# Scores by row quarters and a late division in a chain's cross attention (one NeuronCore)

## The chip, the cores and the metric

One core of a Trainium2 chip runs the whole program in one launch. The metric is device time in microseconds (us), from the first to the last instruction on that core with what lies around them; lower is better. The kernel before takes 2385.2 us in the median of three runs.

## The reference, cut to what matters

Four layers work on `x` of 2 x 1024 tokens and 256 channels, with a context of 2 x 64 tokens and 192 channels. The change lies in layer 0, in its cross attention with 16 heads of 16 channels:

```python
h = _layernorm(x, ln2_w, ln2_b)
q = (h @ q_w + q_b).reshape(B, T, H, HD).transpose(0, 2, 1, 3)
k = (enc @ k_w + k_b).reshape(B, S, H, HD).transpose(0, 2, 1, 3)
v = (enc @ v_w + v_b).reshape(B, S, H, HD).transpose(0, 2, 1, 3)
attn = jnp.einsum('bhtd,bhsd->bhts', q, k) * scale
attn = jnp.where(enc_mask[:, None, None, :], neg, attn)
attn = jax.nn.softmax(attn, axis=-1)
ca = jnp.einsum('bhts,bhsd->bhtd', attn, v).transpose(0, 2, 1, 3).reshape(B, T, C)
x = x + ca @ out_w + out_b
h = _layernorm(x, ln3_w, ln3_b)
h = jax.nn.gelu(h @ mlp1_w + mlp1_b, approximate=False)
x = x + h @ mlp2_w + mlp2_b
```

Here B is 2, T 1024, S 64, C 256, H 16, HD 16. Everything is float32.

## The kernel before

The program runs in parts, one behind another. `part_chain0` (L1065) computes everything between the first self attention and the second one: cross attention, MLP, a routing attention over the 64 context tokens, gates and norms. It works in four blocks; a block is 256 tokens (two tiles `t` of 128 tokens) of each of the two batch rows, which are two streams `s`. `chain_blocks` writes the first and last block out and loops over the middle two. Each stream has its own PSUM tile `ch.ps[s]` of 128 x 2048 floats, which is four banks of 512, so that PSUM is full. Each engine runs its instructions in the order written (`emit` in each engine's block) and waits on semaphores for named steps of other engines (`after`, L784). So the order of the work is the order of the code, on each engine for itself.

One block's cross attention, step by step:

- `head` (L1100, TensorE): turns the norm's output, multiplies by `q_w` (L1109); ScalarE adds the bias and keeps `qT` (L1332). Then the scores (L1117): for each tile `t` and channel half `g` one product of 128 rows with `e.kbd`, 512 columns wide. `kbd` holds the keys of 8 heads side by side, block by block on the diagonal: head `h` of the half uses the rows 16h to 16h+15 and the columns 64h to 64h+63, and everything else is zero. Behind each product a one-instruction product adds the mask's rows (`add_bias`, L876). The steps are `ca.scores0` and `ca.scores1`, one for each tile.
- `cross_vector` (L968, VectorE): for each stream and tile, the maximum over 64 keys per head (L987, "top") and the subtraction (L989, "less"), and one tile later the sums of the exponentials (L976, "total") and their reciprocal, 128 x 16 (L979, "inverse"). Last it copies the turned probabilities of stream 1 out of PSUM (L996, `turned_kept`).
- `cross_scalar` (L1004, ScalarE): the four exponentials (L1009), then the copy of stream 0's turned probabilities (L1012).
- `cross_gpsimd` (L1017, GpSimd): multiplies each tile's exponentials by the reciprocals (L1023, "probs").
- `cross` (L1131, TensorE): in this order `turn(0)`, `values(0)`, `turn(1)`, `projected(0)`, `values(1)`, `projected(1)`. `turn` is 16 transposes into all four banks (L1136). `values` is eight products (L1143), each on 32 columns of the array, four of which run side by side. ScalarE copies the result to `caT` (L1342), and `projected` multiplies it by `o_w` (L1152) and adds a bias row.
- VectorE then runs `finish_block(i - 1)` (the last norm of the block before, L806 to L846; not in block 0), and only then adds the projection to `x` (`ca.x`, L1031) and makes the norm `n3`, with two small steps on GpSimd; TensorE turns it (L883) and starts the MLP (L1217, L1224).

A float32 product shows as two MATMUL records, so the eight products of `values` are 16 records. Of scores and transposes the counts are to be read the same way (a transpose is one record).

## Time and profile before

| | us |
|---|---|
| median of three runs | 2385.2 (2384.72 to 2385.51) |
| the profiled execution, device time | 2383.92 |
| its span, first to last instruction | 2382.2 |
| first chain (blocks 0 to 3), about | 449 to 875 |
| one middle block | 105 |
| mean granted TensorE clock | 0.943 |

PE is TensorE's products, PEld its weight loads, DVE VectorE, ACT ScalarE, POOL GpSimd. Times in the trace are from the start of the span. In a row of the timeline the first number is the start, the second the time that the instructions of the row cover together, then engine, line, operation, output<-input, shapes, count, and in brackets how long the engine had been idle before it and who ended that. The granted clock is given as a share of TensorE's full 2.4 GHz; 0.50 is 1.2 GHz.

### The profile page before, as it was taken

Reading aid. Unit: us, or ns where it says so; the run is one execution under the profiler, and the core shown is the slowest. Engines: PE = TensorE matmul, PEld = TensorE weight load, DVE = VectorE, ACT = ScalarE, POOL = GpSimd, SP = SyncE. Lnnn points to the kernel's source line nnn. Section 1 sums busy time; section 2 is a strip of 40 time slices with the busy share of each in tenths; the row PEclk is TensorE's granted clock in tenths of the full one; section 3 lists DMA queues with packets and bytes.
Section 4 is the critical chain, followed back from the end, with each engine's and each line's share of the span. In section 5 each row is a group of like instructions: output and inputs, shape, how many; then the busy total and the mean of one; then the engine's idle time right before and its main releaser. Section 6 shows DMA issues by size and latency. Waiting matters only on the chain. (4 is left out here: it accounts for less than half of the span.)

```text
span 2382.2 us, 27289 instructions
## 1 busy us (share of the span) xinstructions
PE 2086.4 (88%) x10510; PEld 1203.7 (51%) x10550; DVE 1130.7 (47%) x2031; ACT 933.0 (39%) x1435; POOL 777.5 (33%) x508
## 2 busy tenths in 40 slices
PE   2789998487979767999999999999998979898987
PEld 1444444275757554433343335334433857576766
DVE  5476672435252435455535554555450152525343
ACT  2256665133333322555545553554454422121211
POOL 3211100013032121566646664666466010202011
PEclk8899999699989887999999999999999989899989
DMA  5723320400000004000000000000000500000000
GB/s 121 130 37 44 42 29 2 113 1 0 1 0 0 1 1 122 1 1 1 1 1 1 1 1 1 1 2 1 1 2 1 161 27 1 9 1 9 0 9 9
DMA packets 48266, 52.77 MB, mean 22 GB/s; under 512 B 14730, under 2 KB 39052, under 8 KB 47732
## 3 DMA queue, kind: packets, MB, share of 16 engines
q1 hardware_dynamic: 48148, 51.17, 10.3%
q8 instruction: 77, 1.26, 0.2%
q14 instruction: 41, 0.34, 0.1%
HBM read 41.31 MB, written 8.80 MB: 21 GB/s over the span
## 5 line engine op out<-in xcount | busy, mean ns | idle before, releaser
L1731 POOL TENSOR_TENSOR total<-total,pr 128x1024 f32<-128x1024 f32 x192 | 465.1, 2423 | 241.9 <-ACT pr L1872 229.0
L1872 ACT ACTIVATE pr<-sc 128x1024 f32<-128x1024 f32 x256 | 260.0, 1022 | 355.3 <-PE sc L1651 355.3
L1752 DVE TENSOR_REDUCE pmax<-ring 128x1 f32<-128x512 f32 x512 | 325.9, 685 | 133.9 <-PE ring L1618 125.8
L1669 PE MATMUL o<-pr,v_pair 128*64 128x512 f32 x1024 | 275.7, 617 | 1.2
L1651 PE MATMUL sc<-q_full,k_full 64*128 64x512 f32 x1024 | 267.2, 591 | 0.0
L522 ACT ACTIVATE probs<-s 128x512 f32<-128x512 f32 (+1 forms) x304 | 163.2, 575 | 101.5 <-PE s L309 55.0
L1618 PE MATMUL ring<-k_round,q_round 64*128 64x512 f32 x512 | 185.0, 598 | 5.3 <-DVE pmax L1752 4.3
L1023 POOL TENSOR_TENSOR c_scores<-c_scores,c_total 128x1024 f32<-128x1024 f32 (+1 forms) x48 | 77.0, 1616 | 344.5 <-DVE c_total L979 344.5
L1618 PEld LDWEIGHTS ring<-k_round,q_round 64*128 64x128 f32 x512 | 74.4, 188 | 155.1 <-DVE pmax L1752 97.2
L394 DVE TENSOR_REDUCE row_max<-s 128x1 f32<-128x640 f32 (+3 forms) x128 | 127.3, 1020 | 47.3 <-PE s L291 47.1
L1669 PEld LDWEIGHTS o<-pr,v_pair 128*64 128x64 f32 x1024 | 51.2, 134 | 144.4 <-issue 142.6
L1731 POOL TENSOR_TENSOR total<-pr 128x1024 f32<-128x1024 f32 x32 | 75.3, 2353 | 141.8 <-ACT pr L1872 141.8
L2166 PE MATMUL c_ps<-c_hT,hT 128*128 128x256 f32 x512 | 117.3, 392 | 4.4 <-ACT c_hT L898 4.4
L288 PE MATMUL s<-k_stack,q_stack 128*128 128x512 bf16 (+3 forms) x367 | 92.9, 328 | 30.3 <-DMA k_stack<-mask_dram 16.7
L898 ACT ACTIVATE c_hT<-c_ps,c_ln_b,c_ln_g 128x256 f32<-128x256 f32 x64 | 32.4, 561 | 213.2 <-PE c_ps L883 213.2
L948 PE MATMUL c_ps<-vw,c_pT 128*128 128x256 f32 x384 | 100.0, 421 | 13.3 <-ACT c_pT L1012 13.3
L2166 PEld LDWEIGHTS c_ps<-c_hT,hT 128*128 128x128 f32 x512 | 100.2, 197 | 19.7 <-ACT c_hT L898 5.4
L1648 PE MATMUL sc<-shift,picks 64*128 64x512 bf16 x512 | 104.8, 387 | 4.8 <-DMA shift<-top_dram 4.8
L827 POOL TENSOR_TENSOR c_rstd<-c_moments,eps 128x2 f32<-128x2 f32 x48 | 9.4, 196 | 304.2 <-DVE c_moments L811 304.2
L1651 PEld LDWEIGHTS sc<-q_full,k_full 64*128 64x128 f32 x1024 | 104.6, 192 | 6.9
L306 PE MATMUL s<-q_stack,k_stack 128*128 128x512 bf16 (+3 forms) x361 | 99.3, 325 | 1.2 <-ACT probs L522 0.9
L948 PEld LDWEIGHTS c_ps<-vw,c_pT 128*128 128x128 f32 x384 | 79.8, 213 | 28.4 <-ACT c_pT L1012 15.3
(285 smaller groups left out, 3430.1 us busy)
## 6 DMA issues: line engine op xcount, KB each, us to landing
qk_dram<-qk_parts SPq DMA_DIRECT2D x32, 192.0 KB, 3.1
q_stack<-qk_dram SPq DMA_DIRECT2D x48, 128.0 KB
k_stack<-qk_dram SPq DMA_DIRECT2D x48, 128.0 KB
x<-in_x SPq DMA_DIRECT2D x4, 512.0 KB, 7.3
mlp_w<-in_L_xattn_mlp_w SPq DMA_DIRECT2D x2, 1024.0 KB, 8.1
wq<-in_L_xattn_Wq SPq DMA_DIRECT2D x2, 1024.0 KB, 6.6
wo<-in_L_xattn_Wo SPq DMA_DIRECT2D x2, 1024.0 KB, 14.9
hT<-in_L_xattn_ff_w SPq DMA_DIRECT2D x1, 2048.0 KB, 19.0
```

The lines of the kernel that those rows point to most:

```text
L306: ins = te.matmul(dst[:, x * width:(x + 1) * width], k[:, j, kt * P:(kt + 1) * P], q[:, j, c0:c0 + width], start=True, stop=not diagonal)
L394: dve.tensor_reduce(row_max[:, heads[0], t:t + 1], src[:, 0:(t + 1) * P], AX.X, ALU.max).then_inc(s1_free, 1)
L522: act.activation(probs[at % KEPT][:, heads[0]:heads[-1] + 1, 0:width], s2[u % RING][:, 0:len(heads) * width].rearrange("p (j q) -> p j q", ...
L948: ins = te.matmul(dst, ch.pT[s][:, c, t * P:(t + 1) * P], vw[:, s, c, :], start=c == 0, stop=c == cols // P - 1 and out_bias is None)
L1618: te.matmul(ring[i % RING][:], qr[head[j], t * P:(t + 1) * P], kr[head[j], halves[half]], start=True, stop=True).then_inc(s1_made, 1)
L1648: te.matmul(s2[at % 2][:, j], picks[head[j]], shift[n % 2][head[j], halves[half]], start=True, stop=False)
L1651: ins = te.matmul(s2[at % 2][:, j], kf[n % 2][head[j], keys], qf[n % 2][head[j], halves[half]], start=False, stop=True)
L1669: ins = te.matmul(o[64 * j:64 * j + 64], v[n % 2][:, kt, 64 * j:64 * j + 64], probs[(U * n + u) % KEPT][:, j], start=kt == 0, stop=kt == T ...
L1731: pool.tensor_tensor(out=total[half][:], in0=other[:], in1=probs[at % KEPT][:], op=ALU.add).then_inc(sums, 1)
L1752: dve.tensor_reduce(part_max[:, j, t, half:half + 1], ring[i % RING][:], AX.X, ALU.max).then_inc(s1_free, 1)
L1872: act.activation(probs[here % KEPT][:], s2[at % 2][:], ACT.Exp).then_inc(s2_free, 1)
L2166: ins = te.matmul(ch.ps[s][:, 1024 * part + 256 * f:1024 * part + 256 * (f + 1)], w.f1[:, k, chunk * P:(chunk + 1) * P], ch.hT[s][:, k, :] ...
```

## The change

The scores are computed by row quarters. The 32 rows of quarter `r` hold two heads, whose keys fill 128 columns of `kbd`; the rest of the columns is zero for these rows. Each product of 128 rows and 512 columns becomes four products of 32 rows and 128 columns, one for each quarter `r`, and each quarter writes into its own bank `r` of the stream. The mask's rows are added behind all of them, once for each bank. There is one step `ca.scores` for the four banks in place of two; VectorE reads a tile's 16 heads across all four banks.

The division moves behind the values. VectorE makes no sums over the exponentials and GpSimd multiplies nothing. TensorE turns the bare exponentials, and `values` issues, beside the eight products with the values, eight more with a constant `sums_of`, which put each head's sum on that head's 16 rows, in the third bank. VectorE, behind its copy of stream 1, takes the reciprocal of these 128 x 512 sums and multiplies the 128 x 512 values by it; that is the new `caT`, and ScalarE's copy (L1342) goes. `turn(s)` now waits for "less" of both tiles and the exponential in place of "probs". All of this stands ahead of `finish_block(i - 1)` on VectorE.

```diff
--- before.py
+++ after.py
@@ -651,6 +651,10 @@
         @block.vector
         def _(dve):
             dve.memset(e.vcol[:], 0.0).then_inc(zeroed, 1)
+            dve.memset(e.sums_of[:], 0.0).then_inc(zeroed, 1)
+            dve.wait_ge(zeroed, 2)
+            for x in range(2):
+                dve.memset(e.sums_of[S2 * x:S2 * x + S2, 16 * x:16 * x + 16], 1.0)
...
-            dve.wait_ge(zeroed, 1)
             dve.wait_ge(pe.sem, pe.value("v"))
...
@@ -960,12 +963,15 @@
     return ch.scores[s][:].rearrange("p t n -> p (t n)")[:, 0:2 * cols].rearrange("p (t n) -> p t n", t=2)
 
 
-def cross_vector_steps(name):
+def cross_vector_steps(name, sums=True):
+    if not sums:
+        return [f"{name}.{x}" for x in ("top0", "less0", "top1", "less1", "turned_kept")]
     return [f"{name}.{x}" for x in ("top0", "less0", "top1", "less1", "total0", "inverse0", "total1", "inverse1",
                                     "turned_kept")]
 
 
-def cross_vector(dve, ch, name, i, cols):
+def cross_vector(dve, ch, name, i, cols, quarters=False, sums_made=True):
+
 
     heads = cols // S2
     by_head = lambda ap: ap.rearrange("p (h k) -> p h k", k=S2)
@@ -982,16 +988,23 @@
     last = None
     for s in range(B):
         for t in range(2):
-            src, top = by_head(ch.ps[s][:, t * cols:(t + 1) * cols]), ch.top[s][:, t, 0:heads]
-            after(dve, ch.te[s], f"{name}.scores{t}", i)
+            if quarters:
+                src = ch.ps[s][:].rearrange("p (r t h k) -> p r t h k", r=4, t=2, k=S2)[:, :, t]
+                top = ch.top[s][:, t, 0:heads].rearrange("p (r h) -> p r h", r=4)
+                less, tops = sc(s, t).rearrange("p (r h) k -> p r h k", r=4), top.unsqueeze(3).to_broadcast([P, 4, 4, S2])
+            else:
+                src, top = by_head(ch.ps[s][:, t * cols:(t + 1) * cols]), ch.top[s][:, t, 0:heads]
+                less, tops = sc(s, t), top.unsqueeze(2).to_broadcast([P, heads, S2])
+            after(dve, ch.te[s], f"{name}.scores" + ("" if quarters else str(t)), i)
             dve.tensor_reduce(top, src, AX.X, ALU.max).then_inc(ch.dve[s].sem, ch.dve[s].one(f"{name}.top{t}"))
             after(dve, ch.dve[s], f"{name}.top{t}", i)
-            dve.tensor_tensor(out=sc(s, t), in0=src, in1=top.unsqueeze(2).to_broadcast([P, heads, S2]),
-                              op=ALU.subtract).then_inc(ch.dve[s].sem, ch.dve[s].one(f"{name}.less{t}"))
-            if last:
+            dve.tensor_tensor(out=less, in0=src, in1=tops, op=ALU.subtract).then_inc(
+                ch.dve[s].sem, ch.dve[s].one(f"{name}.less{t}"))
+            if last and sums_made:
                 sums(*last)
             last = (s, t)
-    sums(*last)
+    if sums_made:
+        sums(*last)
     after(dve, ch.te[1], f"{name}.turned", i)
     dve.tensor_copy(ch.pT[1][:, 0:cols // P, :].rearrange("p c n -> p (c n)"), ch.ps[1][:, 0:2 * cols]).then_inc(
         ch.dve[1].sem, ch.dve[1].one(f"{name}.turned_kept"))
@@ -1065,16 +1078,16 @@
 def part_chain0(nc, e, A):
     with ExitStack() as ctx:
         w = e.w0
-        te_steps = ["n2.T", "ca.q", "ca.scores0", "ca.scores1", "ca.turned", "ca.v", "ca.out", "n3.T", "mlp.up", "mlp.down", "n4.T", "rt.scores",
+        te_steps = ["n2.T", "ca.q", "ca.scores", "ca.turned", "ca.v", "ca.out", "n3.T", "mlp.up", "mlp.down", "n4.T", "rt.scores",
                     "rt.turned", "rt.routed", "n5.T", "gates", "cand"]
-        dve_steps = (norm_steps("n2") + cross_vector_steps("ca") + ["ca.x"] + norm_steps("n3")
+        dve_steps = (norm_steps("n2") + cross_vector_steps("ca", False) + ["ca.inverse", "ca.vT", "ca.x"] + norm_steps("n3")
 ...
-        act_steps = ["n2.hT", "ca.qT", *cross_scalar_steps("ca"), "ca.vT", "n3.hT", "mlp.gelu",
+        act_steps = ["n2.hT", "ca.qT", *cross_scalar_steps("ca"), "n3.hT", "mlp.gelu",
                      "x.T", "n4.hT", "rt.exp", "rt.kept", "n5.hT",
                      "r", "u", "tanh"]
         ch = Chain(nc, ctx, "c0", te_steps, dve_steps, act_steps,
-                   ["n2.shifted", "n2.rstd", "ca.probs0", "ca.probs1", "n3.shifted", "n3.rstd", "n4.shifted",
+                   ["n2.shifted", "n2.rstd", "n3.shifted", "n3.rstd", "n4.shifted",
                     "n4.rstd", "n5.shifted", "n5.rstd"], e.biases0.shape[1])
...
+        inverse = ch.sb("inverse", [P, 512])
@@ -1098,8 +1112,8 @@
         @block.tensor
         def _(te):
             def head(i, rows_later=None):
-                scores = lambda s, t, g: ch.ps[s][:, 1024 * t + 512 * g:1024 * t + 512 * (g + 1)]
-                masked = lambda s, t, g: add_bias(te, ch, scores(s, t, g), 4 * C + 512 * s)
+                bank = lambda s, r: ch.ps[s][:, 512 * r:512 * (r + 1)]
+                masked = lambda s, r: add_bias(te, ch, bank(s, r), 4 * C + 512 * s)
                 for s in range(B):
                     turn_step(te, ch, e, i, "n2", s)
                 for s in range(B):
@@ -1112,26 +1126,31 @@
                     ins.then_inc(ch.te[s].sem, ch.te[s].one("ca.q"))
                 for s in range(B):
                     after(te, ch.act[s], "ca.qT", i)
+
                     for t in range(2):
                         for g in range(KC):
-                            te.matmul(scores(s, t, g), qT[s][:, g, t * P:(t + 1) * P], e.kbd[:, s, g, :],
-                                      start=True, stop=False)
-                            if rows_later is None:
-                                ins = masked(s, t, g)
-                        if rows_later is None:
-                            ins.then_inc(ch.te[s].sem, ch.te[s].one(f"ca.scores{t}"))
+                            for r in range(4):
+                                rows = slice(32 * r, 32 * r + 32)
+                                te.matmul(bank(s, r)[:, (2 * t + g) * P:(2 * t + g + 1) * P],
+                                          qT[s][rows, g, t * P:(t + 1) * P],
+                                          e.kbd[rows, s, g, P * r:P * r + P], start=t + g == 0, stop=False)
+                    if rows_later is None:
+                        for r in range(4):
+                            ins = masked(s, r)
+                        ins.then_inc(ch.te[s].sem, ch.te[s].one("ca.scores"))
                 if rows_later is not None:
                     te.wait_ge(ch.rows_made, rows_later)
                     for s in range(B):
-                        for t in range(2):
-                            for g in range(KC):
-                                ins = masked(s, t, g)
-                            ins.then_inc(ch.te[s].sem, ch.te[s].one(f"ca.scores{t}"))
+                        for r in range(4):
+                            ins = masked(s, r)
+                        ins.then_inc(ch.te[s].sem, ch.te[s].one("ca.scores"))
 
             def cross(i):
                 def turn(s):
                     for t in range(2):
-                        after(te, ch.pool[s], f"ca.probs{t}", i)
+
+                        after(te, ch.dve[s], "ca.less1", i)
+                        after(te, ch.act[s], f"ca.exp{t}", i)
                         for c in range(8):
                             ins = te.transpose(ch.ps[s][:, c * 256 + t * P:c * 256 + (t + 1) * P],
                                                ch.scores[s][:, t, c * P:(c + 1) * P], e.ident[:])
@@ -1139,13 +1158,19 @@
 
                 def values(s):
                     after(te, (ch.act, ch.dve)[s][s], "ca.turned_kept", i)
+                    for g in range(KC):
+                        for r in range(4):
+                            ins = te.matmul(ch.ps[s][32 * r:32 * r + 32, 256 * g:256 * (g + 1)],
+                                            e.vcol[:, s, 4 * g + r, :], ch.pT[s][:, 2 * r + g, :],
+                                            start=True, stop=True)
+
                     for c in range(8):
-                        ins = te.matmul(ch.ps[s][32 * (c % 4):32 * (c % 4) + 32, 256 * (c // 4):256 * (c // 4 + 1)],
-                                        e.vcol[:, s, c, :], ch.pT[s][:, c, :], start=True, stop=True)
+                        ins = te.matmul(ch.ps[s][32 * (c % 4):32 * (c % 4) + 32, 1024 + 256 * (c // 4):1280 + 256 * (c // 4)],
+                                        e.sums_of[:], ch.pT[s][:, 2 * (c % 4) + c // 4, :], start=True, stop=True)
                     ins.then_inc(ch.te[s].sem, ch.te[s].one("ca.v"))
 
                 def projected(s):
-                    after(te, ch.act[s], "ca.vT", i)
+                    after(te, ch.dve[s], "ca.vT", i)
                     for t in range(2):
                         dst = ch.ps[s][:, 512 + t * C:512 + (t + 1) * C]
                         for g in range(KC):
@@ -1281,7 +1306,13 @@
                 if first:
                     head(0)
                     assert bias_rows(dve, ch, e.biases0, PIECE) == ROWS_MADE
-                cross_vector(dve, ch, "ca", i, 1024)
+                cross_vector(dve, ch, "ca", i, 1024, quarters=True, sums_made=False)
+                for s in range(B):
+                    after(dve, ch.te[s], "ca.v", i)
+                    dve.reciprocal(inverse[s][:], ch.ps[s][:, 1024:1536]).then_inc(*one(s, "ca.inverse"))
+                    after(dve, ch.dve[s], "ca.inverse", i)
+                    dve.tensor_tensor(out=caT[s][:].rearrange("p g t -> p (g t)"), in0=ch.ps[s][:, 0:512],
+                                      in1=inverse[s][:], op=ALU.mult).then_inc(*one(s, "ca.vT"))
                 if not first:
                     finish_block(i - 1)
                 for s in range(B):
@@ -1338,10 +1369,6 @@
                     head(0)
                 cross_scalar(act, ch, "ca", i, 1024)
                 for s in range(B):
-                    after(act, ch.te[s], "ca.v", i)
-                    act.activation(caT[s][:].rearrange("p g t -> p (g t)"), ch.ps[s][:, 0:512],
-                                   ACT.Identity).then_inc(*one(s, "ca.vT"))
-                for s in range(B):
                     after(act, ch.te[s], "n3.T", i)
                     turned_scalar(act, ch, s, 0, ch.hT[s], w.vec["ln3_g"], w.vec["ln3_b"]).then_inc(*one(s, "n3.hT"))
                 for s in range(B):
@@ -1401,7 +1428,6 @@
             def emit(i, first, last):
                 if first:
                     norm_gpsimd(pool, ch, e, "n2", 0)
-                cross_gpsimd(pool, ch, "ca", i, 1024)
                 if not first:
                     norm_gpsimd(pool, tail, e, "n6", i - 1)
                 for name in ("n3", "n4", "n5"):
@@ -2324,6 +2350,7 @@
         front = ctx.enter_context(ExitStack())
         fb = lambda n, s, d=F32: front.enter_context(nc.sbuf_tensor(n, s, d))
         e.kbd, e.vcol = fb("kbd", [P, B, KC, 512]), fb("vcol", [P, B, 8, 32])
+        e.sums_of = fb("sums_of", [P, 32])
         e.q_w, e.q_bs, e.o_w = fb("q_w", [P, KC, C]), fb("q_bs", [P, KC]), fb("o_w", [P, KC, C])
 
         e.biases0 = fb("biases0", [P, 4 * C + B * 512])
```

## Rows read from the trace of the kernel before

**Rows 1.** The page's busy time of TensorE and its share of the span
```profile
PE 2086.4 (88%) x10510; PEld 1203.7 (51%) x10550; DVE 1130.7 (47%) x2031; ACT 933.0 (39%) x1435; POOL 777.5 (33%) x508
```
**Rows 2.** Windows (length; busy PE, PEld, DVE, ACT, POOL; clock; DMA), blocks 0 and 1
```profile
488.30:573.50 85.20, 78.95 (x389) 61.56 (x388) 31.64 (x82) 30.54 (x65) 16.46 (x23) 1.00 0.00 1
...
573.50:583.80 10.30, 6.16 (x37) 4.08 (x35) 6.38 (x8) 4.65 (x5) 5.66 (x3) 0.50 0.00 0
...
594.00:604.20 10.20, 5.82 (x15) 4.52 (x16) 4.37 (x18) 1.02 (x2) 1.79 (x4) 0.50 0.01 2
```
**Rows 3.** Timeline of PE, block 1, from the first score to the MLP
```profile
562.50 1.02 PE L1117 MATMUL c_ps<-kbd,c_qT 128*128 128x512 f32 x2
563.36 0.38 PE L876 MATMUL c_ps<-c_rows,c_ones 96*128 96x512 bf16 x1
...
573.18 1.64 PE L1136 MATMUL c_ps<-ident,c_scores 128*128 128x128 f32 x8 [1.89 <-POOL c_scores L1023]
...
580.93 1.93 PE L1143 MATMUL c_ps<-c_pT,vcol 128*32 128x256 f32 x16 [2.03 <-ACT c_pT L1012]
582.80 2.44 PE L1136 MATMUL c_ps<-ident,c_scores 128*128 128x128 f32 x16
585.07 1.03 PE L1152 MATMUL c_ps<-o_w,c_caT 128*128 128x256 f32 x4
...
587.62 1.07 PE L1143 MATMUL c_ps<-c_pT,vcol 128*32 128x256 f32 x16 [0.43 <-DVE c_pT L996]
...
597.27 1.11 PE L883 MATMUL c_ps<-ident,c_h 128*128 128x128 f32 x4 [5.65 <-DVE c_h L818]
```
**Rows 4.** Timeline of DVE, block 1: two maxima, copy, start of finish_block, ca.x
```profile
564.86 1.23 DVE L987 TENSOR_REDUCE c_top<-c_ps 128x16 f32<-128x1024 f32 x1 [6.79 <-PE c_ps L876]
...
567.26 1.22 DVE L987 TENSOR_REDUCE c_top<-c_ps 128x16 f32<-128x1024 f32 x1
...
585.27 2.29 DVE L996 COPY c_pT<-c_ps 128x2048 f32<-128x2048 f32 x1 [5.25 <-PE c_ps L1136]
587.49 0.42 DVE L806 BATCH_NORM_STATS2 c_t_stats<-c_xc 128x6 f32<-128x256 f32 x1
...
593.63 0.69 DVE L1031 TENSOR_TENSOR x<-c_ps,x 128x512 f32 x1
```
**Rows 5.** Timeline of ACT, block 1: the last exponential, the copy of stream 0
```profile
577.27 1.06 ACT L1009 ACTIVATE c_scores<-c_scores 128x1024 f32<-128x1024 f32 x1 [2.69 <-DVE c_scores L989]
578.94 1.94 ACT L1012 ACTIVATE c_pT<-c_ps 128x1024 f32<-128x1024 f32 x2 [0.61 <-PE c_ps L1136]
```
**Rows 6.** Groups by form, whole span: VectorE's reciprocals
```profile
L979 DVE RECIPROCAL c_total<-c_total 128x16 f32<-128x16 f32 x32 | 8.1, 253 | 1.1
...
L979 DVE RECIPROCAL c_total<-c_total 128x8 f32<-128x8 f32 x16 | 3.3, 203 | 0.6
L1302 DVE RECIPROCAL c_rtotal<-c_rtotal 128x2 f32<-128x2 f32 x8 | 1.3, 166 | 6.1 <-ACT c_rp L1363 6.1
```
**Rows 7.** Groups by form, first chain alone: what the change removes
```profile
L1023 POOL TENSOR_TENSOR c_scores<-c_scores,c_total 128x1024 f32<-128x1024 f32 x16 | 30.3, 1902 | 56.8 <-DVE c_total L979 56.8
```
**Rows 8.** Timeline of PE: short products, each with its own weight load
```profile
631.68 1.00 PE L1173 MATMUL c_ps<-tokT,c_xT 128*128 128x64 f32 x8
```
**Rows 9.** Weight loads in narrow windows: four column tiles; two row halves (L1651)
```profile
484.27 0.19 PEld L1143 LDWEIGHTS c_ps<-c_pT,vcol 128*32 128x32 f32 x4 [0.23 <-issue]
...
1303.33:1303.53 0.20, 0.20 (x2) 1.00 0.00 0
```
**Rows 10.** Timeline of block 0: the mask's rows, copies of both streams, ca.x
```profile
467.13 1.90 PE L876 MATMUL c_ps<-c_rows,c_ones 96*128 96x512 bf16 x8 [0.45 <-DVE c_rows L862]
...
481.85 1.94 ACT L1012 ACTIVATE c_pT<-c_ps 128x1024 f32<-128x1024 f32 x2 [0.61 <-PE c_ps L1136]
...
488.92 2.29 DVE L996 COPY c_pT<-c_ps 128x2048 f32<-128x2048 f32 x1 [5.99 <-PE c_ps L1136]
...
491.13 0.68 DVE L1031 TENSOR_TENSOR x<-c_ps,x 128x512 f32<-128x512 f32 x1
```

## The prediction

> **What bounds the kernel now.** I read the page first: TensorE is busy 88% of the span [rows 1], so time is mostly won by taking work from it or by closing its gaps. Then the windows of the first chain, where the change lies: its granted clock is full over 85 us of block 0, but in each middle block two stretches of 10 us stand at half, the 1.2 GHz level [rows 2]. The timeline shows what lies ahead of them. TensorE is idle for 1.89 us on GpSimd's multiplication, then 2.03 us on ScalarE's copy; and 5.65 us before the MLP on the norm `n3` [rows 3]. So in the cross attention TensorE is not the bound. The bound is a chain across the engines: scores, softmax on VectorE, exponential, division, turn, copy, values, projection, `ca.x`, norm. Its end is the turn of `n3` at 597.27. VectorE sets that end, because it runs in the order of the code: the copy of stream 1 at 585.27, then `finish_block` from 587.49, then `ca.x` at 593.63 [rows 4]. What I ask of every part of the change is where it puts `ca.x`. Behind it the block goes on as before.
>
> **The change part by part, in a middle block** (times of block 1, 558.95 to 664).
>
> *Scores.* Before, a pair of records takes 0.86 us from its start to the mask product behind it and each mask product 0.22 us more (562.50, 563.36, the next pair at 563.58) [rows 3]. After, a stream has 16 products, 32 records, four of them on different rows of the array. If four run side by side it is eight waves. A wave has 128 columns and a load of its own; the nearest row is eight short products with loads, 1.00 us, so 0.125 us each [rows 8]: 1.0 us in place of 3.44. With four mask products stream 0 is readable at 562.50 + 1.00 + 3 x 0.22 + 0.42 = 564.6, where VectorE began at 564.86 [rows 4]. That is a gain of 0.3 us and no more, because before VectorE needed only the first tile's half. The 4.9 us saved on the two streams turn into idle time. Bounds for the 32 records: 1.0 us (side by side) to 4.0 us (32 x 0.125, one behind another); I take 1.0, since two loads on different row halves fit into 0.20 us together and four on different columns into 0.19 us [rows 9].
>
> *Softmax.* A maximum and a subtraction take 2.40 us (564.86 to 567.26) [rows 4]. Four pairs, with no sums between them, end at 564.6 + 9.6 = 574.2. The last exponential, 1.06 us [rows 5], ends at 575.4. GpSimd's 16 multiplications of 1.90 us [rows 7] go, four of them from each block, and half of those from the path. ScalarE's copy for stream 0 stands behind all four exponentials in its queue, so it ends at 575.4 + 1.94 = 577.4, against 580.9 [rows 5]. This is what the change gains: 3.5 us.
>
> *Values and sums.* At half clock eight products take 1.87 us from the start to the turn behind them (580.93 to 582.80), at full clock 1.07 [rows 3]. The sums are eight more of the same shape. TensorE now idles from about 566 to 569.5 and from 572 to 577.4, longer than the gaps that led to the half clock before, so I take 2 x 1.87 = 3.7: 581.1. The turn of stream 1 takes 2.3 (582.80 to 585.07) [rows 3]: 583.4 against 585.1. The copy on VectorE takes 2.29 [rows 4]: 585.7.
>
> *Reciprocal.* It now works on 512 elements per partition. The rows show 2 elements in 166 ns, 8 in 203, 16 in 253 [rows 6]: 6.2 ns for each further element, over both steps. 253 + 496 x 6.2 ns = 3.33 us. Bounds: 0.69 us, what a plain operation on 128x512 out of PSUM takes (593.63) [rows 4], if the cost did not grow; and 4.0, one such pass on top. I take 3.33, since three sizes lie on one line. With the multiplication, 0.69, it is 4.0 us for a stream: stream 0 has its `caT` at 589.7. On VectorE this replaces nothing; what it replaces is ScalarE's copy. The Trainium skill, VectorE: DVE Perf Modes ("First, the fixed hardware budget"), says that the reciprocal is an iterative divide with a repeat count of 8. Taken as eight cycles of the page's 0.96 GHz for each element, my estimate by that page is 4.27 us and the sum below would be 7.5 us larger; the rows here show 6.2 ns, not 8.3.
>
> *What is queued behind the new waits.* TensorE's order is `turn(1)`, `projected(0)`, `values(1)`, `projected(1)`. Before, ScalarE made `caT(0)` at once and `projected(0)` ran under VectorE's copy. Now VectorE makes it behind that copy, so TensorE waits from 583.4 to 589.7, and `values(1)` waits behind `projected(0)`. Two times 1.03 us [rows 3] is 2.1; a gap of 6.3 us is longer than the one before the MLP, so I take half clock, 4.1: 593.8. Values and sums of stream 1 at full clock again, 1.9: 595.7. Reciprocal and multiplication, 4.0: 599.7. VectorE is in order, so `finish_block` starts only here, in place of 587.49. It takes 6.14 us (587.49 to 593.63) [rows 4]: `ca.x` at 605.9, 12.3 us later than before. `projected(1)` is hidden under it.
>
> *Behind `ca.x`.* Before, the half-clock stretch ended at 604.2 [rows 2], 10.6 us behind `ca.x`. After, TensorE has worked until shortly before (`projected(1)` at 600 to 604), so that stretch should sit a little earlier; I give back 1.1 us. GpSimd's queue has only the norms' small steps left and delays nothing. A middle block costs +11.2 us, and the last one, which has `finish_block(2)` ahead of `ca.x` too, the same: 3 x 11.2 = 33.6.
>
> *Block 0.* It has no `finish_block` at this place. VectorE can begin when four mask products, not two, are through: 467.13 + 0.42 + 3 x 0.22 = 468.2 [rows 10]; +9.6 + 0.1 + 1.06 + 1.94 = 480.9, against 483.8. Values and sums 3.7, turn 2.7 (between the clocks), copy 2.3: 489.6. Then 4.0, projection 3.1, values and sums 2.8, 4.0: 503.5. `ca.x` was at 491.13 [rows 10]: +12.4. Its MLP ran at full clock from the start [rows 2]; after a gap of 4 us under the second reciprocal part of it will not: +1.5. Block 0: +13.9.
>
> *The rest.* The three memsets of `sums_of` lie under loads of weights (price if not: below 0.3 us). The parts behind the chain shift as a whole.
>
> The sum: 33.6 + 13.9 = +47.5 us against the profiled execution's 2383.9, whose span is 2382.2: 2431.4. The median of the runs is 1.3 above that execution, and I forecast **2432 us**.
>
> **The rivals.**
>
> *The row quarters do not run side by side.* Then the stream's scores take 4.0 us in place of 1.0, VectorE begins 3.0 us later in blocks 1 to 3 (block 0's scores are hidden behind the bias rows): +9, 2441 us. For it: the pair of rows with two loads shows that they were in flight together, not that 128 columns of four were. Against it: [rows 9]. The Trainium skill, TensorE: Matmul & The Clock Gate ("LDWEIGHTS (loading the stationary operand)"), says that a load's time goes by its columns, so that 32 rows take as long as 128; that alone would be this rival, but its section on packing small matmuls lets loads on different rows overlap.
>
> *The reciprocal is dearer,* 4.0 us, since it reads PSUM, which no reciprocal of this length here does: eight times 0.67, 2437 us.
>
> *The reciprocal is cheap.* At 0.69 us, eight times 2.64 us fall away from the sum: 21.1 less, 2411 us. For it: no row has a long reciprocal. Against it: three sizes on a line. Even then the order on VectorE keeps it slower.
>
> *The clock stays full: the other side.* The place is TensorE's wait before `values(0)`. If the clock did not fall there or at `projected(0)`, my sum's own half-clock terms go, 1.9 + 2.0 us a block, some 15 in all, and the two old stretches with 6.16 and 5.82 us of busy time at half [rows 2] give up to 6.0 us back in three blocks, 18. With the cheap reciprocal that is 2432 - 21 - 15 - 18 = 2378 us, faster than before; with the reciprocal at 3.33 it would still be about 2399. It decides only if idle gaps of 5 us leave the clock alone and the reciprocal is below about 1.5 us. Against it: gaps of 2 us led to half clock [rows 2, 3].
>
> **How the numbers follow.** A measurement of this kernel can tell about 0.2%, 4.8 us, from no change. Chances: my forecast 0.76, quarters one behind another 0.10, dearer reciprocal 0.06, cheap reciprocal 0.06, full clock with cheap reciprocal 0.02. The forecast's own range is 2422 to 2441: each block has some 2 us of half clock that may fall otherwise. The range takes in the dearer cases and leaves out the last two: 2419 to 2444. Only the last is not slower, and between it and 2390 lies little: faster 0.02, same 0.01, slower 0.97.
>
> **What the changed profile would show.** A RECIPROCAL on 128x512, eight times, near 3.3 us; under 1 us would make me wrong by 20 us. Score records of 32 rows starting in fours, and the two streams through in under 4 us. The first value product about 3.5 us earlier behind the last score than before. TensorE's gap before `projected(0)` near 6 us, released by the multiplication on VectorE. `ca.x` some 12 us later in the block, block length about 116 us. If `ca.x` is not later, the forecast fails; if it is later by 5 us only, the reciprocal was mis-sized.

## The result and the profile after

The changed kernel takes 2434.55 us in the median of four runs (2432.26 to 2436.1), against 2385.11 for the kernel before: ratio 1.0206, 95% interval 1.0194 to 1.0218. It is slower by 49 us. The profiled execution took 2432.26 us, with a span of 2430.4 and a mean granted clock of 0.935 (0.943 before).

The page of the changed kernel, busy time by engine and the granted clock, to be read against [rows 1]:

```profile
PE 2088.7 (86%) x10830; PEld 1207.3 (50%) x10870; DVE 1141.3 (47%) x2018; ACT 927.6 (38%) x1427; POOL 746.6 (31%) x492
...
PEclk8899999688888897899999999999999989998989
```

No engine's busy time says where 48 us went: TensorE has 2 us more, VectorE 11 us more, ScalarE and GpSimd have less work than before. The time is in waits. The groups by form, in the order of the view, name them (after the bar: busy us, mean ns; idle us and who ended it):

```profile
L1177 PE MATMUL c_ps<-o_w,c_caT 128*128 128x256 f32 x64 | 29.9, 620 | 42.4 <-DVE c_caT L1314 42.4
L1312 DVE RECIPROCAL c_inverse<-c_ps 128x512 f32<-128x512 f32 x8 | 26.8, 3353 | 26.8 <-PE c_ps L1168 26.8
...
L1163 PE MATMUL c_ps<-c_pT,vcol 128*32 128x256 f32 x128 | 14.0, 583 | 16.8 <-ACT c_pT L1025 16.8
L1168 PE MATMUL c_ps<-c_pT,sums_of 128*32 128x256 f32 x128 | 11.1, 480 | 0.0
```

The reciprocal of 128x512 takes 3.35 us, eight times. TensorE waits 42.4 us ahead of the projection for VectorE's multiplication, where the kernel before waited 2.9 us for ScalarE's copy. And the projection itself has a mean record of 620 ns, which at full clock is 380: it runs mostly at half clock.

The timeline of TensorE in block 1, which begins at 572.52 (before: 558.95), against [rows 3]:

```profile
576.17 1.17 PE L1134 MATMUL c_ps<-kbd,c_qT 32*128 32x128 f32 x32
577.27 1.04 PE L879 MATMUL c_ps<-c_rows,c_ones 96*128 96x512 bf16 x4
578.24 1.17 PE L1134 MATMUL c_ps<-kbd,c_qT 32*128 32x128 f32 x32
579.35 1.04 PE L879 MATMUL c_ps<-c_rows,c_ones 96*128 96x512 bf16 x4
583.36 2.98 PE L1155 MATMUL c_ps<-ident,c_scores 128*128 128x128 f32 x16 [2.98 <-DVE c_scores L1001]
590.97 1.93 PE L1163 MATMUL c_ps<-c_pT,vcol 128*32 128x256 f32 x16 [4.63 <-ACT c_pT L1025]
592.68 1.93 PE L1168 MATMUL c_ps<-c_pT,sums_of 128*32 128x256 f32 x16
594.54 1.97 PE L1155 MATMUL c_ps<-ident,c_scores 128*128 128x128 f32 x16
602.89 2.07 PE L1177 MATMUL c_ps<-o_w,c_caT 128*128 128x256 f32 x4 [6.37 <-DVE c_caT L1314]
...
607.02 1.62 PE L1163 MATMUL c_ps<-c_pT,vcol 128*32 128x256 f32 x16
608.48 1.04 PE L1168 MATMUL c_ps<-c_pT,sums_of 128*32 128x256 f32 x16
613.73 2.07 PE L1177 MATMUL c_ps<-o_w,c_caT 128*128 128x256 f32 x4 [4.22 <-DVE c_caT L1314]
...
623.38 1.11 PE L886 MATMUL c_ps<-ident,c_h 128*128 128x128 f32 x4 [5.45 <-DVE c_h L821]
```

The quarters do what they are meant to do: 32 records in 1.10 us (576.17 to 577.27) where the scores of one stream took 3.44. Then TensorE has five gaps, of 2.98, 4.63, 6.37, 4.22 and 5.45 us, from the scores to the norm `n3`.

Block 0 differs in two places that the account of the prediction needs, the mask's rows and the start of the MLP:

```profile
466.18 3.60 PE L879 MATMUL c_ps<-c_rows,c_ones 96*128 96x512 bf16 x8 [4.50 <-DVE c_rows L865]
...
510.40 3.72 PE L1242 MATMUL c_ps<-c_hT,mlp_w 128*128 128x256 f32 x16 [1.11 <-ACT c_hT L901]
```

The eight mask products take 3.60 us, after 4.50 us of idle time, where they took 1.90 after 0.45 [rows 10]. The quarters had finished the scores early.

VectorE's timeline of the same stretch, against [rows 4]:

```profile
578.35 1.23 DVE L999 TENSOR_REDUCE c_top<-c_ps 128x16 f32<-128x1024 f32 x1 [6.72 <-PE c_ps L879]
...
586.78 1.23 DVE L1001 TENSOR_TENSOR c_scores<-c_ps,c_top 128x1024 f32<-128x1024 f32 x1
596.55 2.29 DVE L1009 COPY c_pT<-c_ps 128x2048 f32<-128x2048 f32 x1 [8.55 <-PE c_ps L1155]
598.76 3.35 DVE L1312 RECIPROCAL c_inverse<-c_ps 128x512 f32<-128x512 f32 x1
602.14 0.69 DVE L1314 TENSOR_TENSOR c_caT<-c_ps,c_inverse 128x512 f32<-128x512 f32 x1
609.59 3.36 DVE L1312 RECIPROCAL c_inverse<-c_ps 128x512 f32<-128x512 f32 x1 [6.76 <-PE c_ps L1168]
612.98 0.69 DVE L1314 TENSOR_TENSOR c_caT<-c_ps,c_inverse 128x512 f32<-128x512 f32 x1
613.60 0.42 DVE L809 BATCH_NORM_STATS2 c_t_stats<-c_xc 128x6 f32<-128x256 f32 x1
...
619.74 0.68 DVE L1044 TENSOR_TENSOR x<-c_ps,x 128x512 f32 x1
```

`finish_block` begins at 613.60, directly behind the second multiplication, and `ca.x` follows at 619.74. Counted from the start of the block `ca.x` stood at 34.7 us before and stands at 47.2 now: 12.5 us later. VectorE is idle for 8.55 and 6.76 us in between. That is the reading on which the experiments below rest: VectorE is the engine that sets the end, and it is idle for 15 us while it does so.

The windows show the granted clock of the stretches between (0.50 is 1.2 GHz), against [rows 2]:

```profile
580.50:587.50 7.00, 2.98 (x16) 2.43 (x16) 6.90 (x7) 3.17 (x3) 0.00 (x0) 0.77 0.00 0
587.50:594.50 7.00, 3.53 (x32) 1.38 (x32) 0.50 (x1) 2.88 (x3) 0.00 (x0) 0.50 0.00 0
601.00:608.00 7.00, 5.11 (x22) 3.22 (x26) 1.80 (x2) 0.00 (x0) 0.00 (x0) 0.53 0.00 0
608.00:615.00 7.00, 2.78 (x31) 1.65 (x24) 5.38 (x10) 0.00 (x0) 0.00 (x0) 0.74 0.01 2
621.00:628.50 7.50, 4.01 (x11) 3.07 (x12) 3.52 (x15) 1.02 (x2) 1.78 (x4) 0.56 0.00 0
```

The first values and sums, the first projection and the start of the MLP stand at or near half clock, each behind one of the gaps.

### The profile page after: what moved, and what is told of

Its sections match the earlier page's. It is cut to its first block and busy times, and to the rows that moved or that the text cites. A ratio compares the mean times of both kernels' runs of the same rounds, so it can differ in the third digit from the quotient of the medians.

```text
span 2430.4 us, 27885 instructions
## 1 busy us (share of the span) xinstructions
PE 2088.7 (86%) x10830; PEld 1207.3 (50%) x10870; DVE 1141.3 (47%) x2018; ACT 927.6 (38%) x1427; POOL 746.6 (31%) x492
## 5 line engine op out<-in xcount | busy, mean ns | idle before, releaser
L1036 POOL TENSOR_TENSOR c_scores<-c_scores,c_total 128x1024 f32<-128x1024 f32 (+1 forms) x32 | 46.7, 1471 | 287.7 <-DVE c_total L985 287.7
```

## The experiments

The theory was that the whole loss is the late division: a dear reciprocal, placed in VectorE's queue ahead of `finish_block` and `ca.x`, with TensorE's queue waiting behind it. The rivals were that the emptied TensorE loses the time through its clock, that the reciprocal is hidden, and that `finish_block` is in the shadow of something else.

| kernel | median, us | against the kernel before (95%) |
|---|---|---|
| changed kernel | 2434.6 | 1.0206 (1.0194 to 1.0218) |
| quarters only | 2385.4 | 1.0003 (0.9994 to 1.0013) |
| late division only | 2432.5 | 1.0203 (1.0186 to 1.0220) |
| changed, copy for the reciprocal | 2409.1 | 1.0107 (1.0090 to 1.0124) |
| that, and no sum products | 2408.8 | 1.0095 (1.0078 to 1.0112) |
| changed, `finish_block` early | 2408.3 | 1.0102 (1.0085 to 1.0119) |
| that, and stream 0 divided before the copy | 2381.7 | 0.9984 (0.9974 to 0.9994) |
| before, `finish_block` early | 2367.9 | 0.9924 (0.9908 to 0.9941) |
| changed, quarters in turn | 2443.4 | one run |

Each ratio is to runs of the kernel before on the same chip. Their median was 2385.1 us for the changed kernel; 2384.4 for quarters only, late division only, the copy and `finish_block` early in the changed kernel; 2385.9 for the rest. A difference between two medians of the table therefore carries up to 1.5 us from the chips, beside the spread of the runs. Where this matters I also give the length of the chain in the profiled executions, from the first product with `q_w` in block 0 to the first MLP product behind the turn of stream 1's `n3` in block 3: 362.3 us before and 409.4 us in the changed kernel.

**Each part alone.** Quarters only: the kernel before with the new `head`, `quarters=True` in `cross_vector` and the new order of chunks in `values`.

```diff
-                cross_vector(dve, ch, "ca", i, 1024)
+                cross_vector(dve, ch, "ca", i, 1024, quarters=True)
```

> The scores by row quarters alone; sums, reciprocals and GpSimd's multiplication as before. Theory (the late division on VectorE's queue costs everything, the quarters only empty TensorE): within 4 us of before, 2383 to 2389; the two streams' scores through in 4.1 us in place of 8.6, and GpSimd's first multiplication at most 0.3 us earlier in the block. Rival (the emptied TensorE costs time through its clock): 2395 or more, with a third half-clock stretch in each block.

Late division only: the changed kernel with the old `head` and the old order of chunks in `values`.

```diff
-                cross_vector(dve, ch, "ca", i, 1024, quarters=True, sums_made=False)
+                cross_vector(dve, ch, "ca", i, 1024, sums_made=False)
```

> The late division alone; scores as before. Theory: all of the loss is here, 2428 to 2437. Rival (the emptied TensorE and its clock): the scores keep TensorE busy 4.5 us longer in each block, so the first values run at full clock and the loss shrinks by 2 us or more a block: 2425 or less.

Measured: 2385.4 and 2432.5. The quarters alone cannot be told from no change, and the late division alone has the whole loss: its interval and the changed kernel's cover each other. The timeline of TensorE in the kernel with the quarters only shows why 4.6 us of freed TensorE bring nothing:

```profile
565.17 1.17 PE L1130 MATMUL c_ps<-kbd,c_qT 32*128 32x128 f32 x32
...
567.24 1.17 PE L1130 MATMUL c_ps<-kbd,c_qT 32*128 32x128 f32 x32
568.35 1.04 PE L876 MATMUL c_ps<-c_rows,c_ones 96*128 96x512 bf16 x4
575.67 1.97 PE L1149 MATMUL c_ps<-ident,c_scores 128*128 128x128 f32 x8 [6.28 <-POOL c_scores L1033]
```

The scores of both streams are through in 4.2 us (565.17 to 569.39) in place of 8.8, and the next instruction of TensorE then waits 6.28 us for GpSimd in place of 1.89 [rows 3]. The rival with the clock would have needed 2395 us or more; at that size it falls for the quarters. A small part of it is there: in block 0 the eight mask products take 3.60 us in place of 1.90, after 4.29 us of idle time, and that block is 105.6 us long in place of 104.1, which the medians cannot resolve. In the kernel with the late division only TensorE worked on its scores until the turn of stream 0, and its first values were hardly faster for it (1.83 us for the 16 records, against 1.93), so that rival falls there too. Both medians lie in the ranges expected of them.

**The reciprocal's share.** The division is left out of this kernel: it multiplies the values by the sums.

```diff
-                    dve.reciprocal(inverse[s][:], ch.ps[s][:, 1024:1536]).then_inc(*one(s, "ca.inverse"))
+                    dve.tensor_copy(inverse[s][:], ch.ps[s][:, 1024:1536]).then_inc(*one(s, "ca.inverse"))
```

> The changed kernel with a copy of 128x512 in place of the reciprocal; the output is then not divided by the sums, but multiplied by them. Theory: eight times 3.35 - 0.6 us fall off the path, 22 us: 2410 to 2415, so that the rest of the loss, some 27 us, is the queue's order, the sums and the clock. Rival (the reciprocal is mostly hidden and the order of the queues costs all): above 2425.

Measured: 2409.1, 25.4 us less than the changed kernel. This is just below the expected range of 2410 to 2415, and the four runs spread from 2405.4 to 2413.6. The copy takes 0.69 us, so the durations explain 8 x (3.35 - 0.69) = 21.3 us; in the profiled executions the chain is 20.4 us shorter (388.9 in place of 409.4). So the reciprocals were on the path with nearly their whole time, and the rest of the 25.4 us lies outside the chain or in the scatter of the runs. The timeline of TensorE in block 1 shows that the clock moves both ways:

```profile
593.18 1.13 PE L1177 MATMUL c_ps<-o_w,c_caT 128*128 128x256 f32 x4 [3.71 <-DVE c_caT L1314]
...
594.26 1.79 PE L1177 MATMUL c_ps<-o_w,c_caT 128*128 128x256 f32 x4
...
612.31 6.65 PE L1242 MATMUL c_ps<-c_hT,mlp_w 128*128 128x256 f32 x16 [1.11 <-ACT c_hT L901]
```

The gap ahead of the first projection is 3.71 us in place of 6.37, and the first half of the projection still finds the full clock (1.13 us against 2.07). But the gap ahead of the MLP's transposes grows from 5.45 to 7.43 us, and the first 16 MLP records take 6.65 us in place of 5.22. Block 1 is 4.8 us shorter (112.12 in place of 116.95), a little less than the 5.3 of two reciprocals.

**The sums' share.** The same kernel without the eight sum products; the values are then multiplied by numbers left in PSUM.

```diff
-                    for c in range(8):
-                        ins = te.matmul(ch.ps[s][32 * (c % 4):32 * (c % 4) + 32, 1024 + 256 * (c // 4):1280 + 256 * (c // 4)],
-                                        e.sums_of[:], ch.pT[s][:, 2 * (c % 4) + c // 4, :], start=True, stop=True)
```

> e3_no_reciprocal without the eight sum products a stream either; the output is then the values times stale numbers in PSUM. Theory: the sums stand on the path for 1.9 us at half clock for stream 0 and 0.9 us at full for stream 1: 2.7 us a block, 11 us in all below e3: 2396 to 2401. Rival (the sums are hidden or cost only at full clock): 2403 or more.

Measured: 2408.8, against 2409.1 with the sums. The two kernels ran on different chips; by their ratios (1.0095 and 1.0107) the difference is 2.9 us, and the intervals leave room for several us to either side. The expectation of 11 us was wrong. The timeline of TensorE in its block 1:

```profile
583.89 1.94 PE L1163 MATMUL c_ps<-c_pT,vcol 128*32 128x256 f32 x16 [4.33 <-ACT c_pT L1025]
585.75 2.53 PE L1155 MATMUL c_ps<-ident,c_scores 128*128 128x128 f32 x16
592.00 2.08 PE L1173 MATMUL c_ps<-o_w,c_caT 128*128 128x256 f32 x4 [3.71 <-DVE c_caT L1310]
...
611.13 5.26 PE L1238 MATMUL c_ps<-c_hT,mlp_w 128*128 128x256 f32 x16 [1.11 <-ACT c_hT L901]
```

The turn behind the values now starts 1.7 us earlier (1.86 us behind the start of the values, with the sums 3.57), but it takes 2.53 us in place of 1.97, the first part of it at half clock, where with the sums it had the full clock throughout; and the projection runs at half clock (2.08), where its first half had the full clock with the sums (1.13). Its windows over the turn and over the projection have the clocks 0.75 and 0.50; with the sums the same two stretches have 0.99 and 0.70:

```profile
585.75:588.20 2.45, 2.45 (x20) 2.30 (x16) 0.00 (x0) 0.00 (x0) 0.00 (x0) 0.75 0.00 0
592.00:596.10 4.10, 4.10 (x10) 2.70 (x10) 0.00 (x0) 0.00 (x0) 0.00 (x0) 0.50 0.00 0
```

In this block `ca.x` comes 1.1 us sooner after the block's start, where the expectation had 2.7; the rest was given back in clock. The start of the MLP is faster on top of that (5.26 us against 6.65), so that the block as a whole is 2.5 us shorter (109.6 against 112.1). Blocks 0 and 2 are 3.1 and 1.2 us shorter, and the chain is 6.5 us shorter (382.5 against 388.9). The span hides it: in this execution the chain starts 3.1 us later, with no change ahead of it, and the part behind it takes 2.8 us longer, 1.7 of them because the first eight records of the second self attention run slower (5.37 us against 3.67). With one profiled execution of each kernel it is not shown which of this would come again. What holds by every measure is that the sums cost less than their forecast 11 us; whether it is 0.3 (the medians), 2.9 (the ratios) or 6.5 (the chain) stays open. The starts of the first chain differ by up to 4.3 us between the profiled executions (452.8 to 457.1).

**Do the quarters run side by side?** The quarter becomes the outermost loop.

```diff
-                    for t in range(2):
-                        for g in range(KC):
-                            for r in range(4):
-                                rows = slice(32 * r, 32 * r + 32)
+                    for r in range(4):
+                        rows = slice(32 * r, 32 * r + 32)
+                        for t in range(2):
+                            for g in range(KC):
```

> The changed kernel with the quarter as the outermost loop of the scores, so that four products on the same 32 rows follow one another in place of four on different rows. Theory (the 1.1 us for 32 records is four quarters side by side): the 32 records take 2 us or more, up to 4.0, and each of blocks 1 to 3 is 1 to 3 us longer: 2437 to 2443. Rival (a product of 32 rows is short by itself, whatever its neighbours): 1.1 us again, 2432 to 2436.

Measured, in one run: 2443.4. The timeline of TensorE:

```profile
577.12 2.82 PE L1134 MATMUL c_ps<-kbd,c_qT 32*128 32x128 f32 x32
579.87 1.04 PE L879 MATMUL c_ps<-c_rows,c_ones 96*128 96x512 bf16 x4
```

The same 32 records take 2.75 us in place of 1.10 when neighbours share their rows. So a product of 32 rows is not short by itself, and the order in which the products are issued decides how long they take. The run is just above the expected 2437 to 2443, and block 1 is 3.2 us longer (120.14 against 116.95): 1.65 of it is there at the first values, the rest lies in slower records behind them (the second turn 2.82 us against 1.97, the second values 1.94 against 1.62). In this kernel the quarter also picks the PSUM bank, so that neighbours on the same rows write into the same bank too. That four quarters run side by side is shown; that it is the rows and not the banks that keep the others apart is not.

**VectorE's order.** `cross_vector` gets a hook ahead of the copy of stream 1, and `finish_block(i - 1)` goes there.

```diff
+    if between:
+        between()
     after(dve, ch.te[1], f"{name}.turned", i)
     dve.tensor_copy(ch.pT[1][:, 0:cols // P, :].rearrange("p c n -> p (c n)"), ch.ps[1][:, 0:2 * cols]).then_inc(
...
-                if not first:
-                    finish_block(i - 1)
```

> The changed kernel with finish_block(i - 1) moved into VectorE's idle time ahead of the copy of stream 1 (8.5 us idle there, 6.1 needed). Theory (VectorE's order sets ca.x): 6.1 us less in each of three blocks, and TensorE's gap before the MLP closes, so up to 3 us more of clock each: 2407 to 2416. Rival (the chain through TensorE and PSUM sets the MLP's start anyway, finish_block was in its shadow): 2428 or more.

Measured: 2408.3, 26 us less than the changed kernel. 18.4 of it are the three norms themselves. In the profiled executions the chain is 23.4 us shorter, and block 1 is 8.2: 6.1 are the norm, and most of the rest is the gap ahead of the MLP, which its timeline of TensorE shows closed, with the MLP at full clock from its first record (3.72 us for 16 records against 5.22):

```profile
616.92 1.11 PE L886 MATMUL c_ps<-ident,c_h 128*128 128x128 f32 x4 [0.31 <-DVE c_h L821]
619.15 3.72 PE L1244 MATMUL c_ps<-c_hT,mlp_w 128*128 128x256 f32 x16 [1.11 <-ACT c_hT L901]
```

Then, in addition, stream 0 is divided ahead of the copy of stream 1:

```diff
+    if divide:
+        divide(0)
     after(dve, ch.te[1], f"{name}.turned", i)
```

> e4_finish_early, and besides the division of stream 0 moved ahead of the copy of stream 1 on VectorE, so that projected(0) follows turn(1) sooner. Theory: the first division starts when the first sums are made, about 2 us before the turn of stream 1 ends; TensorE's 6.4 us gap before projected(0) shrinks to some 2.5, so 2 to 5 us less in each of four blocks than e4: 2388 to 2402, still slower than before. Rival (the copy of stream 1 is then late and values(1) waits for it as long): 2404 or more.

Measured: 2381.7, another 26.5 us less, and now just faster than the kernel before. The expectation's 2388 to 2402 was too slow: it had the shorter gap but not what the gap does to the clock. In block 1 `ca.x` comes 6.0 us sooner than with `finish_block` early alone: the projection starts 3.7 us sooner and takes 1.9 us less. TensorE's timeline:

```profile
593.77 1.13 PE L1181 MATMUL c_ps<-o_w,c_caT 128*128 128x256 f32 x4 [1.14 <-DVE c_caT L1317]
...
595.96 1.07 PE L1167 MATMUL c_ps<-c_pT,vcol 128*32 128x256 f32 x16
596.85 1.05 PE L1172 MATMUL c_ps<-c_pT,sums_of 128*32 128x256 f32 x16
```

The gap ahead of the first projection is 1.14 us in place of 6.37, and this projection and the values and sums of stream 1 are at full clock: 1.13 against 2.07 for half a projection. The values and sums of stream 0 still take 1.93 us each, and the second projection still begins at half clock (2.04).

**A version that beats both.** The same move of `finish_block` in the kernel before, with nothing else changed.

> The kernel before, with only finish_block(i - 1) moved ahead of VectorE's copy of stream 1, where VectorE is idle for 5.25 us. GpSimd ends its last multiplication at 582.5, so the moved norm waits for it and the copy may come some 2 us later; ca.x then follows the copy directly. Theory (VectorE's order sets ca.x): 3 to 4 us less in each of three blocks, and up to 3 us of clock each, since TensorE's gap of 5.65 us ahead of the MLP nearly closes: 2366 to 2377, faster than before. Rival (the delayed copy gives it all back): 2382 to 2388.

Measured: 2367.9, ratio 0.9924 (0.9908 to 0.9941), 18.0 us less than the kernel before, in four runs from 2363.6 to 2369.1. The timeline of VectorE:

```profile
586.08 0.88 DVE L839 SCALAR_TENSOR_TENSOR c_t_h<-c_xc,c_t_moments,r_o_g 128x256 f32<-128x256 f32 x2 [1.76 <-POOL c_t_rstd L830]
...
589.54 2.28 DVE L998 COPY c_pT<-c_ps 128x2048 f32<-128x2048 f32 x1
591.74 0.68 DVE L1033 TENSOR_TENSOR x<-c_ps,x 128x512 f32 x1
```

The norm waits 1.76 us for GpSimd, as expected, and the copy of stream 1 is late for it; but `ca.x` follows the copy directly, and stands 30.2 us behind the block's start in place of 34.7. A block is 98 us long in place of 105: some 4.5 us are VectorE's order, and the other 2.6 lie at the start of the MLP, whose half-clock stretch is gone (16 records in 3.72 us in place of 6.07). Its windows of block 1 have a mean granted clock of 0.95, those of the kernel before 0.90:

```profile
561.57:659.50 97.93, 85.91 (x428) 66.63 (x428) 42.92 (x109) 35.11 (x71) 23.91 (x31) 0.95 0.00 1
```

## Why the prediction was right

The forecast was 2432 us, the range 2419 to 2444; measured 2434.6. (The prediction's own sum is 2431.4 + 1.3 = 2432.7.) The mechanism holds in the middle blocks; in block 0 two errors cancel. Point by point, in times from the start of block 1:

*Scores and softmax.* Forecast 1.0 us for 32 records, measured 1.10. VectorE began 5.83 us into the block, forecast 5.6 (before 5.91). The rival in which the quarters run one behind another falls, by the rows and by the kernel with the quarters in turn. Two of the signs were worded wrongly: both streams' scores are through in 4.2 us, not in under 4 (the prediction's own parts add up to 3.8), and the first value product comes 3.5 us earlier in the block, but behind the last score it comes later (10.6 us against 9.6), since the scores end 4.6 us sooner. The Trainium skill, TensorE: Matmul & The Clock Gate ("Part 3: Packing small matmuls"), says that loads for different row groups overlap with running products; the 1.10 us agree. What the prediction cites of its section on LDWEIGHTS holds here for a single load (187 ns for 32 rows, 190 for 128) and is no bound when four go to different rows.

*First values.* Forecast 577.4, which is 18.45 us into the block; measured 590.97, again 18.45. The gain of 3.5 us was there and was the whole gain. They ran at half clock, 1.93 us, as taken (1.87).

*Reciprocal.* Forecast 3.33 us from three sizes of 2 to 16 elements, measured 3.35 at 512: 6.25 ns for each further element, (3353 - 253) / 496. The dearer and the cheap reciprocal fall. The estimate that the prediction made from the Trainium skill (VectorE: DVE Perf Modes, "First, the fixed hardware budget"), its repeat count of 8 read as eight cycles of 0.96 GHz an element, was 4.27 us; the trace does not agree.

*Queued behind it.* `caT(0)` was forecast 30.75 us into the block and came at 30.3 (602.14 + 0.69); TensorE's gap was forecast at 6.3 and is 6.37; the projection at half clock, as taken. The second reciprocal was to begin at 36.75 and began at 37.07, because half of the second values still ran at half clock. `finish_block`: forecast 40.75, measured 41.08; `ca.x`: 46.95, measured 47.22.

*Behind `ca.x`.* I gave back 1.1 us a block for an earlier end of the half-clock stretch. In block 1 `ca.x` was 12.5 us late and the first MLP product behind the turn of stream 1's `n3` 11.7 us: 0.8 given back.

*The sum.* Block 0 was forecast at +13.9 and came 14.5 us later to its end; the three others at +11.2 each and came +11.9, +10.3 and, the last one with all that follows, +12.4. The start of the chain differed by 0.9 us the other way: 14.5 + 11.9 + 10.3 + 12.4 - 0.9 = 48.2, the difference of the spans. The middle blocks are alike in their code, so I take the difference between 11.9 and 10.3 for clock, as the spread of 2 us in the forecast had it. Of the 12.4, 2.1 lie behind the chain, in the part that was forecast to shift as a whole; 1.7 of them are the first eight records of the second self attention (5.37 us in place of 3.67).

Block 0 came out near its forecast by luck. Its `ca.x` was forecast 12.4 us later and came 13.9 us later: VectorE began 0.8 us later than forecast, because the mask's rows ran slower behind TensorE's wait (3.60 us in place of 1.90), and the first projection took 4.1 us, half clock, where the forecast took 3.1. The +1.5 us that the forecast put on the MLP did not come: its first 16 records took 3.72 us, as before. The one error pays for the other.

What the prediction did not have right is what one of its terms is worth. It had the sums on the path with 1.87 us at half clock and 0.86 at full for the two streams of a block, 11 us in all. The kernel without them is less than that faster (0.3 to 6.5 us, depending on the measure), because the clock behind them is in part worse. The forecast came out since it was made with the sums in place.

The rival on the other side, clock kept full and a cheap reciprocal, was wrong in both halves. That the clock has a price is shown by the two moves in VectorE's order, which brought 52.9 us (2434.6 to 2381.7) with the same reciprocals and sums. Block 1 became 14.5 us shorter by them: 6.2 are the norm, 4.1 the earlier start of the projection, and some 4.3 the clock (projection 1.9, values and sums of stream 1 0.6, start of the MLP 1.8). The rival had priced the clock at 9.9 us in a middle block.

## What to carry to other kernels

Before a division is moved, look up what its reciprocal costs for each element in the trace's own rows and multiply by the new count: 32 elements per partition became 512, and 6.2 ns each turned reciprocals of 0.25 us into 3.35 us twice a block on the path. Then read the queue of the engine that gets the new work to its end: what is written behind the new wait (`finish_block` and `ca.x` here) waits too, even where the engine is idle for 15 us. Work of no urgency belongs into such an idle stretch; moving it there was worth 18.0 us, 0.8%, on the old kernel, more than the 3.5 us a block that the change gained.

## What the runs showed of the hardware that I had not expected

Taking work off TensorE need not bring its time, even on the path. Without the eight sum products of stream 0 the turn behind the values starts 1.7 us earlier, but the projection only 1.1 us, since the turn takes 2.53 us in place of 1.97; and the projection itself then runs at half clock from its start (2.08 us against 1.13 for its first half).

Four products of 32 rows and 128 columns on different rows, each with its own load of 128 columns, run at 34 ns a record (1.10 us for 32); the same records with neighbours on the same rows, and in the same bank, at 86 ns (2.75 us).
